# Two-layer graph network on one core: the gather's last adjacency panel goes to the first one's place, and GpSimd forms the five sums of weight blocks

## The reference

```python
h   = relu(x @ W_self0 + mean(x) @ W_neigh0 + b0)      # mean over incoming edges
y   = layernorm(x + h @ W_self1 + mean(h) @ W_neigh1 + b1)
g   = norm-weighted sum over neighbours of y (each node is its own neighbour too)
out = layernorm(y + g @ W.T + (scale of the row) * b)
```

## Time and profile before

| | |
|---|---|
| median of 3 runs | 853.41 us (853.07 to 855.98) |
| the profiled execution's own time | 852.77 us |
| its span in the trace | 851.0 us |
| mean granted TensorE clock | 0.992 of full speed |
| TensorE matmul busy | 97% of the span |
| VectorE busy | 59% |
| ScalarE busy | 23% |
| GpSimd busy | 54%, all of it before 66% of the span |

### The profile page before, as it was taken

The page is one execution under the profiler, slowest core; times in us unless marked ns, Lnnn a source line. Parts: engine busy times, 40 slices in busy tenths (PEclk is TensorE's granted clock), DMA queues, the critical chain, the costliest instruction groups (busy, mean ns, idle before and its releaser), DMA issues.

```text
span 851.0 us, 11076 instructions
## 1 busy us (share of the span) xinstructions
PE 827.3 (97%) x4271; PEld 705.7 (83%) x4271; DVE 502.6 (59%) x778; ACT 196.2 (23%) x245; POOL 456.9 (54%) x343
## 2 busy tenths in 40 slices
PE   8999999999999999999999999999999996999996
PEld 6888888888898899788888888778889896988885
DVE  6465659200018566897553687766656554579986
ACT  5111131111111113443213012222222332212110
POOL 4028777787777788885888788787600000000000
PEclk9999999999999999999999999999999997999999
DMA  9977965453786433868886578268767589797771
GB/s 328 379 305 277 349 194 156 136 164 87 200 258 166 116 88 98 292 238 285 281 287 222 208 270 269 48 192 228 221 206 265 152 245 336 237 364 273 250 240 71
DMA packets 113401, 191.02 MB, mean 224 GB/s; under 512 B 15826, under 2 KB 86490, under 8 KB 108480
## 3 DMA queue, kind: packets, MB, share of 16 engines
q1 hardware_dynamic: 63696, 131.51, 46.0%
q10 hardware_dynamic: 37264, 43.80, 15.1%
q0 software_dynamic: 12384, 14.95, 7.6%
HBM read 114.42 MB, written 75.58 MB: 223 GB/s over the span
## 4 chain that ended last, share of the span: by engine, by line
PE 85%; DMA 5%; DVE 5%; ACT 2%; issue 1%; ACTq 1%; SPq 0%; DVEq 0%
PE ps L1854 19%; PE ps L1711 17%; PE ps L1766 12%; PE ps L1889 10%; PE ps L1871 9%; PE ps L1797 8%; PE ps L1944 4%; PE ps L1740 2%; DMA spare<-in_x 1%; DMA u<-adj_out 1%; PE ps L1695 1%; DMA xin<-s0t_scr 1%; DVE u L1078 1%; ACT outb L865 1%; PE ps L1652 1%
## 5 line engine op out<-in xcount | busy, mean ns | idle before, releaser
L747 POOL DMA_INDIRECT adj_out<-loops,idx_out x160 | 244.0, 1525 | 65.0 <-issue 65.0
L747 POOL DMA_INDIRECT adj_in<-mult,idx_in x160 | 197.2, 1232 | 86.4 <-issue 86.4
L1854 PE MATMUL ps<-u 128*128 128x512 f32 x840 | 190.7, 389 | 1.4 <-DVE u L1078 1.4
L1854 PEld LDWEIGHTS ps<-u 128*128 128x128 f32 x840 | 157.6, 188 | 34.3 <-issue 1.6
L1766 PE MATMUL ps<-wx 128*128 128x512 f32 (+1 forms) x576 | 109.4, 351 | 1.5 <-ACT outb L865 1.5
L1766 PEld LDWEIGHTS ps<-wx 128*128 128x128 f32 x576 | 93.9, 189 | 17.1 <-ACT outb L865 2.1
L1871 PE MATMUL ps<-u,panel_tiles 128*128 128x512 f32 (+1 forms) x400 | 93.9, 393 | 1.8 <-DVE u L1078 1.8
L1797 PE MATMUL ps<-wx,u 128*128 128x256 f32 (+5 forms) x640 | 94.8, 309 | 0.3 <-DVE ht L1357 0.3
L1797 PEld LDWEIGHTS ps<-wx,u 128*128 128x128 f32 (+1 forms) x640 | 86.6, 191 | 7.3 <-DVE ht L1357 0.7
L1711 PE MATMUL ps<-wx 128*128 128x512 f32 x384 | 89.6, 392 | 0.0
L1871 PEld LDWEIGHTS ps<-u,panel_tiles 128*128 128x128 f32 (+1 forms) x400 | 74.5, 188 | 18.0 <-issue 2.2
(11 more groups left out here) (218 smaller groups left out, 930.9 us busy)
## 6 DMA issues: line engine op xcount, KB each, us to landing
left_scr<-u SPq DMA_DIRECT2D x7, 2560.0 KB, 9.4
u<-left_scr SPq DMA_DIRECT2D x7, 2560.0 KB, 9.8
xt_scr<-wx ACTq DMA_DIRECT2D x10, 1024.0 KB, 10.6
wx<-xt_scr SPq DMA_DIRECT2D x16, 512.0 KB, 4.0
u<-halves_scr SPq DMA_DIRECT2D x14, 512.0 KB, 4.7
adj_in<-u POOLq DMA_DIRECT2D x4, 1600.0 KB, 25.2
adj_out<-u POOLq DMA_DIRECT2D x4, 1600.0 KB, 14.5
wx<-adj_in SPq DMA_DIRECT2D x5, 1280.0 KB, 7.0
```

What stands on the lines that cost most here:

```text
L747: pool.indirect_dma_start(table, bass.IndirectOffsetOnAxis(ap=index[0:EP, j:j + 1], axis=0), counts[0:EP, j:j + 1], None, bounds_check=CEL ...
L1854: ins = nc.tensor.matmul(ps[:, product_bank(g, i, p), :], left_op[n % 2][:, p, k, left, :], right_op[n % 2][:, k, right, :], start=(not on ...
```

## The change

The place of chunk 3's panel becomes chunk 0's (m2_panels[3]). The SP queue loads it as soon as chunk 0 is done, before weight rows 3 to 6; row 7 is loaded ahead of the two left tiles and not behind the bias. Rows 5, 6 and 7 of the weights may now be split once chunk 1 is done, so the splits stand at m = 4, 9, 13, 16, 19, 22, 25, 28 where before six stood at 4, 9, 13, 16, 20, 24 and two behind the gather. The load of the residual rows now waits for all four chunks' s_step. The five sums of weight blocks are formed by GpSimd with tensor_tensor, and ScalarE waits for them on pool_set.

```diff
         m2_panels = [panels_at(panel_tiles, PER, 1), panels_at(u_flat, XT_AT - 2 * PSIZE, 2), panels_at(u_flat, XT_AT, 1),
-                     panels_at(u_flat, XT_AT - PSIZE, 1)]
+                     panels_at(panel_tiles, PER, 1)]
...
                 if c == 3:
-                    sp.wait_ge(g_full, KD * 2)
-                    sp.wait_ge(s_step, NT * 2)
+                    sp.wait_ge(g_full, KD)
+                    sp.wait_ge(s_step, NT)
                 load_panels(adj_out, c, m2_panels[c], m2_full)
-                for k in {1: (2, 3), 2: (4, 5), 3: (6,)}[c]:
+                for k in {1: (2,), 2: (), 3: (3, 4, 5, 6)}[c]:
                     sp.wait_ge(w_lo_done, KD * GCN + k - 1)
                     load_w(GCN, k)
...
+            sp.wait_ge(w_lo_done, KD * GCN + 6)
+            load_w(GCN, 7)
             sp.wait_ge(g_full, KD * 3)
             sp.wait_ge(s_step, NT * 3)
...
             sp.dma_start(bias[:, :], b_gcn.rearrange("(a d) -> a d", a=1).broadcast_to([P, D])).then_inc(bias_full, 16)
-            sp.wait_ge(w_lo_done, KD * GCN + 6)
-            load_w(GCN, 7)
             sp.wait_ge(g_full, KD * 4)
-            sp.wait_ge(s_step, NT)
+            sp.wait_ge(s_step, NT * 4)
...
+            for i, j, op, out_of in ((0, 1, ALU.subtract, 0), (2, 1, ALU.add, 1), (3, 2, ALU.subtract, 2), (2, 0, ALU.add, 3), (3, 1, ALU.add, 4)):
+                pool.wait_ge(block_in[i], 48)
+                pool.wait_ge(block_in[j], 48)
+                nc.gpsimd.tensor_tensor(sums_whole[out_of][:, :, 1, :], w_block[i], w_block[j], op).then_inc(pool_set, 1)
...
-                elif l == GCN and k == 5:
+                elif l == GCN:
                     act.wait_ge(g_full, 2 * KD)
                     act.wait_ge(s_step, 2 * NT)
-                elif l == GCN:
-                    act.wait_ge(g_full, 32)
-                    act.wait_ge(s_step, 4 * NT)
...
-                if m in (4, 9, 13, 16, 20, 24):
-                    split_hi(GCN, (4, 9, 13, 16, 20, 24).index(m))
+                if m in (4, 9, 13, 16, 19, 22, 25, 28):
+                    split_hi(GCN, (4, 9, 13, 16, 19, 22, 25, 28).index(m))
             store_g(31)
-            split_hi(GCN, 6)
-            split_hi(GCN, 7)
...
-                act.wait_ge(right_sum, 9 + x)
+                act.wait_ge(pool_set, 4 + x)
```

More of the change, by code:

```diff
@@ L1520, in _ @@
                     scale_done(c)
[L1521 to L1524, removed]
+                if m in (4, 9, 13, 16, 19, 22, 25, 28):
+                    split_lo(GCN, (4, 9, 13, 16, 19, 22, 25, 28).index(m))
             after = [0]
@@ L1555, in plain @@
                     half_stats(t % 2, n)
[L1557 to L1561, removed]
             def sum_low(x):
@@ L1608, in _ @@
             add_rest(1)
-            weight_sum(0)
-            weight_sum(1)
             finished(0)
-            weight_sum(2)
             add_rest(8)
-            weight_sum(3)
             finished(1)
-            weight_sum(4)
             sum_low(0)
```

## The result

The changed kernel takes 857.39 us (median of 5 runs, 856.75 to 858.21) against 853.41 us before: a ratio of 1.0042, 95% interval 1.0027 to 1.0057. It is slower by about 0.4%, where a gain of 9 us was forecast. The profiled execution took 856.75 us, its span 855.1 us, 4.1 us more than before.

What follows compares the result with a forecast made beforehand. TensorE, with 85% of the chain, was taken to bound the kernel: 852.77 - 5.59 - 2.83 - 1.0 = 843.35 at best, taken as 843.6, plus 0.64 for the median gives 844.2 us; range 842.6 to 848.0.

Steps and rivals of the forecast that it cites:

- Part 1, the panel: Gather, before chunk 3: early panel load removes the 5.59 us hole and 2.8 us of slow clock, -8.4 us so far.
- Part 2, the split at m = 19: End of chunk 2: about 1.1 us of VectorE work ahead of the panel sums; unchanged evictions would raise TensorE's wait to 2.1.
- Part 3, the traffic: Gather: moved panel transfers shift ScalarE's evictions at 704.85 by -3 to +1 us, taken as -2, saving TensorE's 1.0 us wait.
- The store at 664: Store ScalarE awaits until 666.74, 1.89 us before the change; forecast 1 to 4 us later beside the moved panels.
- the issue pair at 680: Two ScalarE issues at 680.67 took 5.21 us beside chunk 2's panel; forecast 2.8 at most, saving 2.4 or more, taken as 3.
- rival (a): ScalarE's lag stays or grows; TensorE waits 2 to 4 us between chunks 2 and 3: 846 to 849 us, chance 0.15.
- the 9.4: Forecast gather savings at best: 5.59 us hole, 2.83 us slow clock and 1.0 us panel-sum wait.
- Part 4, the left tiles: SP queue before the plain tiles: tiles issued at 716 to 719, tile 0 there 2 to 5 us early, cost nothing.
- Part 5, the sums: Strassen rounds: moving five sums to GpSimd spares VectorE 11.4 us but is worth 0, at about 4.5 us a sum.
- the bound of 8.5 us: Strassen rounds: TensorE waits at product 6 only if one GpSimd sum costs over 8.5 us.
- Rival (c): GpSimd and VectorE obstruct each other; stretched sums over 8.5 us delay product 6; chance 0.04, half slower by over 0.5%.
- 20 us of room: Strassen rounds, before product 6: claimed slack for the GpSimd sums at 4.5 us each.

Runs made afterwards that it cites:

- the copies first: The changed kernel with ScalarE's first two copies of half products ahead of tile 7's square root: 859.60 us, ratio 1.0048 to the kernel before.
- the panel alone: The changed kernel with its five weight sums back on VectorE: 850.59 us, ratio 0.9954 to the kernel before.
- the panel behind the store: Changed kernel, sums on VectorE, chunk 2's first six panel sums early, chunk 3's panel issued after block 7's store landed: 846.54 us, 0.9902 to the kernel before.

## Why the prediction was wrong

**Part 1, the panel: right.** It was issued at 656.42, no wait for adj_out is left, and the gather's old hole of 5.59 us is gone. The slow clock of chunk 3 was 2.6 us (20.69 against 18.11 in a run at full clock), forecast 2.83. But I wrote that a hole of the next size "costs only itself", from one row after 1.8 us of idleness. The holes of 2.1 to 2.55 us at chunk 2's end were followed by a granted clock of 0.50 to 0.71 in the next 2 us, and chunk 3 took 19.7 instead of 18.1 us: 1.6 us came back (2.6 in the run with the copies first). Nor does the size of a hole decide alone. The hole of the row that I had read, before the first matmuls of L1871 (L1863 in both runs here), was 1.84 us with the copies first and 2.13 with the panel alone, and the clock fell behind the shorter one:

```profile
536.38:538.38 2.00, 2.00 (x5) 1.60 (x6) 2.00 (x4) 2.00 (x2) 1.70 (x2) 0.56 0.06 1
```

```profile
536.71:538.71 2.00, 2.00 (x9) 1.65 (x10) 2.00 (x4) 2.00 (x2) 1.70 (x2) 1.00 0.06 1
```

The first cost 1.6 us (80 matmuls in 20.20 us instead of 18.60). What decides it isn't shown. Such falls come in some executions of a kernel and not in others, and they are part of why its runs differ by some microseconds (the mean granted clock of the six runs of the panel behind the store goes from 0.993 to 0.999).

**Part 2, the split at m = 19: half right.** Its 1.1 us is in the wait (1.0 to 2.3 us), but with the split moved back the wait stays, since a store takes its place.

**Part 3, the traffic: the sizes came out at the bad end.** The store at 664 waited 4.1 us more (I said 1 to 4 and took about 1), the issue pair at 680 went from 5.21 to 2.55 us as forecast, and evictions of chunk 2 started at 705.28 and not at 702.8. That was rival (a), and it cost 2.3 + 1.6 = 3.9 us of the 9.4: the gather gave 5.5. So the forecast of 844.2 was too low even without the sums: the panel alone comes to 849.5 us by its ratio. The run with the panel behind the store shows that the 9.4 us were there.

**Part 4, the left tiles: right.** Issued at 718.97, landed 7.7 us later, well ahead of 734.6.

**Part 5, the sums: this is the step that failed.** It said that TensorE doesn't wait for VectorE there, so the move is worth nothing, and that TensorE waits only if one sum costs GpSimd over 8.5 us. The move cost 6.6 us of hole and 2.9 us of clock, with a sum at 4.69 us.

My price of a sum was right, in part by luck: 4.5 us was the rate of another operation, a select of 128 numbers, carried over to 2048. The Trainium skill, "GPSIMD Engine Reference", section 3.1, has 4497 ns; the trace, with 4.69 us, is 4% above both. But the bound of 8.5 us was for the sums' own readiness, and what a sum does to VectorE's other instructions I had put at nothing. Rival (c), with a chance of 0.04, named the two engines getting in each other's way, but priced only a stretched sum that makes product 6 late. The runs showed the reverse: the sum kept its length, VectorE's small instructions were stretched, VectorE lost 19 us and got 11.4 back, and product 2 was late.

And the cover was not what I had taken it for. I gave the fifth sum 20 us of room, but the path that decides is tile 7's square root on ScalarE and the copy behind it, and that had 0.4 us. VectorE had hardly any idle time from 752 to 800 before; a wait list of TensorE that names no VectorE there doesn't show how near it was.

The Trainium skill, "GPSIMD Engine Reference", section 8, says that GpSimd shares its SBUF interfaces with VectorE and contends with those of its instructions that have two SBUF inputs or run in a two-port mode. The traces agree in which instructions are held: those with two SBUF inputs and the 1024-wide TENSOR_SCALAR, not the reciprocal, the statistics, the one-element TENSOR_SCALAR, nor the form with a PSUM input. They show besides that the wait lasts to the end of the GpSimd instruction under way.

## What to carry to other kernels

Before work goes from a nearly full engine to one that shares its way into memory, price the longest single instruction there as a wait that each dependent small instruction of the first engine may pay; if it must go, cut it in short pieces. Ask first what the move can gain: here, even in pieces, nothing that could be measured. Room is not where the moved result is read but on the tightest path through the engine that gives it up: take the time of each message it sends (here a square root and the copy queued behind it) against the time at which it is needed. And a transfer moved into an idle stretch of the DMA engines still meets the one small store that somebody waits for.

## What the runs showed of the hardware

- One VectorE TENSOR_TENSOR over one number per partition took 0.16 us alone, up to 4.53 us beside GpSimd instructions of 4.7 us, and up to 1.21 us beside instructions of 1.5 us.
- A two-input GpSimd TENSOR_TENSOR over 128x2048 fp32 took 4.69 us; four over 128x512 took 4 x 1.50 = 6.0 us, both with VectorE at work beside them.
- A DMA store of 256 KB that ScalarE waits for delayed it 1.9 us with the engines nearly idle, 2.1 us behind one panel of 1.28 MB that another queue had issued 8.5 us earlier, and 6.0 us behind two.
- Behind TensorE's holes of 2.32 and 3.04 us the granted clock was 0.51 and 0.50 (1.2 GHz), behind holes of 1.69 and 1.72 us 1.00 (2.4 GHz). In between there is no fixed border in these runs: 0.56 behind one of 1.84 us, 1.00 behind one of 2.13.
